# Moving GpSimd's low part of x ahead of the band and the chain's link in each step

## The reference

```python
y = einsum('nchw,dc->ndhw', gn(x), Wp) + bp          # 256 -> 512 channels: 8 heads x (32 point + 32 value)
# each head and each quarter of an image (64 x 64 pixels) is its own problem with 64 centres
center = block_means(y)                               # 8 x 8 centres
sim    = sigmoid(alpha * cos(x_point, c_point) + beta)
max_v, max_i = sim.max(2), sim.argmax(2)
agg    = cat(c_value, 1).at[max_i].add(max_v * cat(x_value, 1))
agg    = agg[:, :-1] / agg[:, -1:]
x      = x + einsum(max_v * agg[max_i], Wm) + bm
# layer 1
s      = sigmoid(relu(mean_dct(gn(x)) @ w1.T) @ w2.T)  # one factor per image and channel
out    = x + gn(x) * s
```

## Time and profile before

| | us |
|---|---|
| median of 3 runs | 4877.42 (4873.61 to 4877.58) |
| the profiled execution, own time | 4864.42 |
| its span in the profile | 4862.7 |

### The profile page before, as it was taken

The page is one execution under the profiler, slowest core; times in us unless marked ns, Lnnn a source line. Parts: engine busy times, 40 slices in busy tenths (PEclk is TensorE's granted clock), DMA queues, the critical chain, the costliest instruction groups (busy, mean ns, idle before and its releaser), DMA issues.

```text
span 4862.7 us, 141670 instructions
## 1 busy us (share of the span) xinstructions
PE 4446.0 (91%) x51792; PEld 4264.2 (88%) x51792; DVE 3599.0 (74%) x7894; ACT 3328.0 (68%) x8843; POOL 3219.9 (66%) x3519
## 2 busy tenths in 40 slices
PE   1888999999999999999999999999999999999950
PEld 1788899999999999999999999999999999999940
DVE  3766788887887778787888778887887867777740
ACT  4666677777777777776777777777777766666621
POOL 1455566677777777776777777777777767777640
PEclk9999999999999999999999999999999999999985
DMA  5444455576877777777877767787777766666548
GB/s 169 112 102 111 112 123 127 134 187 163 188 190 184 178 176 186 185 188 164 186 190 187 182 166 189 184 187 171 183 189 183 182 142 155 158 152 157 123 123 202
DMA packets 1852770, 798.84 MB, mean 164 GB/s; under 512 B 1663008, under 2 KB 1663408, under 8 KB 1852080
## 3 DMA queue, kind: packets, MB, share of 16 engines
q1 hardware_dynamic: 1852080, 789.77, 67.7%
HBM read 395.15 MB, written 260.05 MB: 135 GB/s over the span
## 4 chain that ended last, share of the span: by engine, by line
PE 69%; POOL 13%; issue 6%; POOLq 3%; DMA 3%; ACT 2%; SPq 2%; DVE 1%; ACTq 0%; DVEq 0%
PE bank L1040 47%; PE bank L1201 7%; PE bank L1145 6%; PE bank L1188 4%; POOL xl L644 3%; PE bank L1175 3%; POOL dl L655 2%; POOL vals L651 2%; DMA chunk<-x 2%; POOL vpart L598 2%; POOL fin L604 2%; SPq L355 1%; DMA out<-fin 1%; ACT xh L793 1%; ACT ysq L784 1%
## 5 line engine op out<-in xcount | busy, mean ns | idle before, releaser
L644 POOL TENSOR_TENSOR xl<-xr,xh 128x512 fp32r<-128x512 f32 x512 | 654.5, 1278 | 584.0 <-ACT xh L793 569.5
L651 POOL TENSOR_TENSOR vals<-vals,vpart 128x528 f32<-128x528 f32 x512 | 614.8, 1201 | 519.1 <-ACT vpart L829 518.8
L943 DVE TENSOR_TENSOR gath<-bank,mv 128x512 f32<-128x512 f32 x512 | 353.9, 691 | 642.7 <-PE bank L1145 641.7
L931 DVE TENSOR_REDUCE rank<-bank 128x8 f32<-128x512 f32 x1024 | 694.1, 689 | 94.2 <-PE bank L1040 81.4
L655 POOL TENSOR_TENSOR dl<-dsq,dh 128x512 fp32r<-128x512 f32 x512 | 661.1, 1291 | 53.9 <-ACT dsq L831 53.7
L768 ACT ACTIVATE yh<-bank,bpf 128x256 fp32r<-128x256 f32 x1024 | 428.7, 469 | 364.2 <-PE bank L1040 363.3
L1040 PE MATMUL bank<-xh,wph 128*128 128x256 f32 x2048 | 583.4, 285 | 93.1 <-POOL xl L644 60.0
L803 ACT ACTIVATE dh<-bank 128x512 fp32r<-128x512 f32 x512 | 305.2, 596 | 525.4 <-PE bank L1175 525.1
L952 DVE TENSOR_TENSOR hot<-bank,rank 128x512 bf16<-128x512 f32 x1024 | 654.9, 681 | 0.0
L598 POOL TENSOR_TENSOR vpart<-vals,vpart 128x528 bf16<-128x528 f32 x512 | 611.4, 1194 | 64.0 <-ACT vpart L762 63.9
L1040 PE MATMUL bank<-ch,yh 128*128 128x256 f32 x2048 | 621.0, 303 | 0.0
(11 more groups left out here) (169 smaller groups left out, 13183.3 us busy)
## 6 DMA issues: line engine op xcount, KB each, us to landing
chunk<-x SPq DMA_DIRECT2D x512, 256.0 KB, 3.8
xr<-x SPq DMA_DIRECT2D x1024, 128.0 KB, 2.5
mixed<-xr SPq DMA_DIRECT2D x480, 256.0 KB, 2.6
fin<-mixed SPq DMA_DIRECT2D x480, 256.0 KB, 3.7
out<-fin SPq DMA_DIRECT2D x960, 128.0 KB, 3.3
hot_t<-hot SPq DMA_TRANSPOSE x1024, 2.5
out<-xr SPq DMA_DIRECT2D x64, 128.0 KB, 2.8
wraw<-wp_t SPq DMA_DIRECT2D x1, 512.0 KB, 4.0
```

Of the source, the lines that this page charges most:

```text
L644: pool.tensor_tensor(xl[:, G0 % 2], xr[:, G0 % SLOTS], xh[:, G0 % 2].bitcast(F32), ALU.subtract).then_inc(s_xl, 1)
L651: pool.tensor_tensor(vals[:, G2 % 2], vals[:, G2 % 2], vpart[:, 0], ALU.subtract).then_inc(s_r1, 1)
L931: op = V.tensor_reduce(rank[:, t], sims[t], axis=AX.X, op=ALU.max)
L943: V.tensor_tensor(gath[:, :].rearrange("p (a c) -> p a c", c=CH), g_ps[:, :].rearrange("p (a c) -> p a c", c=CH), mv[:, J1 % SIGS].rearran ...
```

## The change

GpSimd's subtraction for `xl`, with its wait for `s_xh`, is issued right after the third part of the values, ahead of the band and of all links of the step. Nothing else is changed: the same instructions run, on the same engines.

```diff
@@ -596,6 +596,10 @@
                 if on(G3):
                     pool.wait_ge(s_v2, upto(G3))
                     pool.tensor_tensor(vpart[:, 2], vals[:, G3 % 2], vpart[:, 1], ALU.subtract).then_inc(s_v3, 1)
+                if on(G0):
+                    pool.wait_ge(s_xh, upto(G0))
+                    pool.tensor_tensor(xl[:, G0 % 2], xr[:, G0 % SLOTS], xh[:, G0 % 2].bitcast(F32),
+                                       ALU.subtract).then_inc(s_xl, 1)
                 for n, b in scale_at(i):
                     u = n * BANDS + b
                     pool.wait_ge(s_ab, upto(n))
@@ -639,10 +643,6 @@
                 R = (i - 1 + CENTRE_LEAD) // GROUPS
                 if (i - 1 + CENTRE_LEAD) % GROUPS == 0 and R < 4 * N and R % 4:
                     centres_low(R)
-                if on(G0):
-                    pool.wait_ge(s_xh, upto(G0))
-                    pool.tensor_tensor(xl[:, G0 % 2], xr[:, G0 % SLOTS], xh[:, G0 % 2].bitcast(F32),
-                                       ALU.subtract).then_inc(s_xl, 1)
                 for half in range(2):
                     if (i - half) % PER == 0 and PER <= i - half < NG:
                         weights_low((i - half) // PER, half)
```

## The result

The changed kernel takes 5068.74 us in the median against 4877.5 before, a ratio of 1.040, 95% interval 1.037 to 1.042. It is slower, as forecast, but by 191 us instead of 153, and the time lies 4 us above the upper end of the range. The profiled execution took 5067.0 us (span 5065.3), 202.6 more than the profiled one before.

What follows compares the result with a forecast made beforehand. The prediction took TensorE, full in ordinary steps, as the bound. Delays of 102 us plus 51 us for the clock gave 153; 4864.4 + 153 + 13 = 5030 us, range 4965 to 5065.

Steps and rivals of the forecast that it cites:

- table steps with a band (26): Steps from 99 on in which GpSimd runs table_mean behind xl and band: 26 x 2.44 us lost, 63 us.
- table steps without (5): The 5 earlier table_mean steps, which have no band: about 1 us lost each, 5 us.
- fold and centres: GpSimd's link work behind xl makes dl late for the next mixing: 8 us; bounds 20 gain to 25 loss.
- Ordinary steps: Steps with TensorE full: xl starts when xh is there either way, the delay behind it goes unseen; 0 us.
- Table steps, the delay: In table_mean steps den comes 3.74 us late, holding back yl, norms and similarities: 63 plus 5 us.
- Gate chain, the delay: GpSimd's image_sums 3.16 us late, TensorE waiting, 21 us; gate_input 2.57 late, 0.7 us each, 5 us.
- The clock: TensorE's clock falls behind the long new gaps: 32 x 1.6 = 51 us, bounds 0 and 90.
- Rival with full clock (0.27): The delays come but TensorE's clock stays up: 4877 + 102 = 4979 us; chance 0.27.
- Rival in which the waits simply go (0.06): TensorE's 61.4 us of xl waits vanish and GpSimd's queue catches up in time: 4816 us; chance 0.06.
- Its point of decision: In table_mean steps, the xl waits simply vanish if den is late by less than 1.3 us; the rows give 3.74.
- Falling further behind (0.06): GpSimd lags for several steps after each special step, late dl costing more: above 5065 us; chance 0.06.

Runs made afterwards that it cites:

- the filled kernel: Changed kernel plus matmuls of no use in TensorE's new gaps (table, image_sums and gate_input steps): 4965.2 us, ratio 1.0191 to the kernel before.
- the last experiment: Kernel before with xl moved only behind den or gate_input, image_sums ahead of the band, nine matmuls of no use in each fold: 4838.98 us, ratio 0.9928.
- the split kernel: Kernel before with table_mean cut behind den and the next addition, xl put there; in gate_input steps xl ahead of the centres' low part: 4844.6 us, ratio 0.9941.
- the band first: Changed kernel with the band put back ahead of xl in all steps: 4974.04 us, ratio 1.0214 to the kernel before.

## Why the prediction was right and wrong

The terms against what the filled kernel (delay: it against the kernel before) and the changed kernel (clock: it against the filled one) lost by the steps, in us:

| term | delay forecast | delay measured | clock forecast | clock measured |
|---|---|---|---|---|
| table steps with a band (26) | 63 | 58.5 | 42 | 53.8 |
| table steps without (5) | 5 | 4.6 | 0 | 12.0 |
| image_sums | 21 | 21.3 | 10 | 17.7 |
| gate_input | 5 | 4.1 | 0 | 10.0 |
| fold and centres | 8 | 5.4 | 0 | 11.0 |
| start of the run and ordinary steps | 0 | 9.0 | 0 | -6.1 |
| sum | 102 | 103 | 51 | 98 |

- **Ordinary steps: right.** From step 64 on, 222 steps stand clear of the table, gate, fold and centres' steps and of those just behind them; together they take as long as in the kernel before, to 0.01 us. `xl` starts when `xh` is there, in both.
- **Table steps, the delay: right**, and by the mechanism named: `xh`, `xl`, band, table, `den`, `yl`, norms. Of the 4.5 us less, some 3 are the third regions: VectorE's wait for `den` was 1.45 us there in the kernel before already, against 1.03 in the others, so less was lost. The rest is 0.1 to 0.4 us that each following step gives back.
- **Gate chain, the delay: right.** TensorE's wait in the `image_sums` step (L1049) was 3.77 us against 0.55 in the earlier trace rows; it and the one in the `gate_input` step (L1091), from the changed kernel's timeline of TensorE:

```profile
3266.12 0.56 PE L1049 MATMUL bank<-small,gsum 128*128 128x4 f32 x2 [3.77 <-POOL small L558]
...
3288.32 0.24 PE L1091 MATMUL bank<-small,w1s 128*16 128x1 f32 x4 [2.53 <-POOL small L565]
```

- **Fold and centres: right in size** as a delay. Steps 319 and 320, where the centres' low part is pushed behind `xl` and holds back `dl`, lost most of it (TensorE waits 0.91 us for `dl` there). The 11.0 us in the clock's column are another matter. Nearly all of them stand in the two steps of each fold with the slow stretch of the last experiment. The kernel before has that stretch too, the filled kernel has no fill there, and without any edit at the fold these two steps took 21.7 us in one execution and 23.3 in another, against 25.2 in most images of the changed kernel. What share of the 11.0 the change caused isn't shown.
- **The clock: the step that failed.** The mechanism was right and its size was not: it had 1.6 us for each of 32 gaps, 51 us in all; it measured 98, of which 93.5 in the steps of the new gaps. Two things were mis-sized. First, which gaps: only those of 3.7 us and more were counted, because the steady state showed none between 1.6 and that and the start's rows began at 3.3. The clock fell as well behind those of 2.1 to 2.5 us, in the five table steps without a band and in the `gate_input` steps: 22 us where the table has 0. Second, the length: seven of eight gaps in the start had cost it, 1.6 us on the average; here all of them did, 53.8 / 26 = 2.1 us behind a table step and 17.7 / 7 = 2.5 behind the sums. From their first to their last slow weight load the slow stretches are 3.1 to 6.4 us long behind the table steps and 5.3 behind the sums (2.3 in the first image), where the eight at the start ran from none at all to 5.7. Taking the mean of eight scattered gaps at the start for steps that repeat one pattern was the error; the upper bound of 2.8 us each over 32 gaps (90 us) lay nearer, but left the short gaps out. The range was also narrower than its own bounds: 25 instead of 8 for the fold makes 119 us of delays, and 4877 + 119 + 90 = 5086 us, not 5065.
- **A row that was at hand and not used.** The prediction says that waits of up to 1.6 us in the steady state cost no clock. That is wrong: in the kernel before, half clock follows the fold's gap of 1.11 us in six of seven images (the row from 2838.00 to 2842.00 above). It would have spoken for a loss behind short gaps.
- **Rival with full clock (0.27): wrong**, 4979 us; it is what the filled kernel makes (4965). **Rival in which the waits simply go (0.06): wrong.** Its point of decision was confirmed from the other side by the split kernel: with `den` not late, the removal of y's waits does gain, though 29 us and not 61. **Falling further behind (0.06): the time was in its reach, the mechanism wasn't;** GpSimd recovers within two steps.

## What to carry over

An instruction that waits for its input takes that wait along to wherever it is moved: before moving it up, list what it overtakes and who waits for each of these, and cut a long piece behind the one result that another engine wants. A wait moved onto TensorE has two prices, its length and the clock behind it, and in this kernel the second was nearly as large as the first; matmuls of no use in a gap tell the two apart, and can stay in where they pay, as they did in the long gaps here. A stretch that comes and goes from one execution to the next can't be credited to an edit by one trace: look for it in the traces of kernels that leave that place alone. When one wait is removed, look for the next that stood in its shadow before counting its full length as gain.

## What was not expected of the hardware

From step 51 on, the granted clock of the changed kernel fell to 0.5 behind every one of its waits of 2.08 to 4.17 us for the norms, the sums and `gate_input`, 42 in all. The shortest, with the stretch behind it:

```profile
4462.02 0.24 PE L1091 MATMUL bank<-small,w1s 128*16 128x1 f32 x4 [2.08 <-POOL small L565]
4462.00:4466.00 4.00, 3.98 (x24) 3.98 (x25) 1.55 (x3) 0.60 (x1) 3.63 (x6) 0.61 0.27 94
```

Matmuls whose result nobody reads kept it at 1.00. But the length of the gap alone doesn't decide it. Gaps of 2.4 us passed at full clock four times in 29 with the band first. In the kernel before, from step 51 on, none of the seven gaps of 1.3 to 1.6 us was followed by half clock, and the fold's gap of 1.11 us was, in six of seven images. What decides between these cases isn't shown here.
